# Turning z in 32x32 blocks on VectorE instead of 128x128 tiles on TensorE, in an attention and mixture kernel on one core

## The reference

```python
x = x + attn(layernorm(x))          # 32 heads of 128, 8 key/value heads, chunks of 128 tokens
# per head and chunk: y = (q k^T * decay) v + (q * exp(G)) state ; state = state * dec + k_dec^T v
# y = y / rms(y) * gnorm_w * silu(gate)          -> this is z, up to gnorm_w
# attn = z.reshape(B, L, 32 * 128) @ Wo.T
x = x + ffn(layernorm(x))           # dense 512x512 plus 8 experts of rank 16, softmax weights
```

## Time and profile before

| | |
|---|---|
| median of 3 runs | 1987.81 us (1986.06 to 1990.85) |
| the profiled execution, its own time | 1986.23 us |
| its span | 1984.4 us |
| mean granted TensorE clock | 0.986 of full speed |
| PE busy | 1899.7 us, 96% of the span |
| DVE / ACT / POOL busy | 60% / 38% / 33% |
| DMA | 173.63 MB, 27.2% of 16 engines' time |

### The profile page before, as it was taken

One profiled execution on the slowest core, in us unless ns is written; L12 is line 12 of the kernel. 1 busy time (PEld: TensorE's weight loads), 2 busy tenths in 40 slices (PEclk: granted clock), 3 DMA queues, 4 the chain that ended last, 5 costly groups with the idle time before them and its releaser, 6 DMA issues. The chain is left out here.

```text
span 1984.4 us, 28939 instructions
## 1 busy us (share of the span) xinstructions
PE 1899.7 (96%) x9240; PEld 1514.9 (76%) x9240; DVE 1183.8 (60%) x2208; ACT 759.0 (38%) x2326; POOL 658.1 (33%) x741
## 2 busy tenths in 40 slices
PE   7799999999999999999999899999978999999998
PEld 5588788778877877887788788788766777777775
DVE  7767666766676677666666766766664333333322
ACT  4444444444444444444444444444453121111211
POOL 3443444434444444444444444344410110100100
PEclk9899999999999999999999999999999999999999
DMA  4231222223222222322221232222255322322311
GB/s 150 69 96 59 89 98 70 64 83 100 75 80 98 69 67 84 105 65 92 92 73 61 81 102 72 83 75 68 81 191 176 107 89 70 106 66 92 104 54 43
DMA packets 88389, 173.63 MB, mean 87 GB/s; under 512 B 9392, under 2 KB 15024, under 8 KB 88240
## 3 DMA queue, kind: packets, MB, share of 16 engines
q1 hardware_dynamic: 88240, 171.81, 27.2%
HBM read 133.50 MB, written 38.27 MB: 87 GB/s over the span
## 5 line engine op out<-in xcount | busy, mean ns | idle before, releaser
L82 PE MATMUL p_proj<-wg_hi,shared 128*128 128x512 f32 x1024 | 361.0, 433 | 0.0
L82 PE MATMUL p_proj<-shared,wq_hi 128*128 128x512 f32 x992 | 335.9, 400 | 12.3 <-DVE wq_lo L747 12.3
L111 POOL TENSOR_TENSOR q<-rope_a,rope_b 128x512 f32<-128x512 f32 x128 | 181.5, 1418 | 326.7 <-DVE rope_b L103 326.7
L899 ACT ACTIVATE tanh<-p_proj 128x512 f32<-128x512 f32 x128 | 76.5, 598 | 531.1 <-PE p_proj L82 531.1
L82 PEld LDWEIGHTS p_proj<-wg_hi,shared 128*128 128x128 f32 x1024 | 192.9, 188 | 84.5 <-issue 46.3
L82 PEld LDWEIGHTS p_proj<-shared,wq_hi 128*128 128x128 f32 x992 | 187.1, 189 | 57.7 <-issue 15.1
L82 PE MATMUL p_proj<-wg_lo,shared 128*128 128x512 f32 x512 | 202.2, 395 | 0.0
L82 PE MATMUL p_proj<-shared,wq_lo 128*128 128x512 f32 x496 | 196.3, 396 | 0.0
L101 DVE TENSOR_TENSOR rope_a<-p_proj,cos 128x512 f32<-128x512 f32 x155 | 105.8, 683 | 128.6 <-PE p_proj L82 128.6
L680 PE MATMUL p_y<-v_tok,probs 128*128 128x128 f32 x1024 | 182.3, 275 | 0.0
L82 PE MATMUL p_proj<-shared,wkv_hi 128*128 128x512 f32 x496 | 175.2, 415 | 5.2 <-DVE rope_b L103 4.5
(11 more groups left out here) (181 smaller groups left out, 3795.7 us busy)
## 6 DMA issues: line engine op xcount, KB each, us to landing
g_row<-g_scratch SPq DMA_DIRECT2D x128, 256.0 KB, 3.9
z_scratch<-z_t SPq DMA_DIRECT2D x128, 256.0 KB, 2.8
w_raw<-z_scratch SPq DMA_DIRECT2D x49, 512.0 KB, 6.5
e_row<-e_scratch SPq DMA_DIRECT2D x96, 256.0 KB, 3.6
w_raw<-in_wq_t SPq DMA_DIRECT2D x16, 512.0 KB, 6.0
w_raw<-in_wg_t SPq DMA_DIRECT2D x16, 512.0 KB, 6.0
q<-z_scratch SPq DMA_DIRECT2D x15, 512.0 KB, 6.6
w_raw<-in_wo_t SPq DMA_DIRECT2D x11, 512.0 KB, 4.2
```

Of the source, the lines that this page charges most:

```text
L82: mm = pe.matmul(out, lhs[a], rhs[e], start=(i == 0 and j == 0), stop=(i == len(pairs) - 1 and j == 2))
L111: pool.tensor_tensor(out, keep["rope_a"][:, s, :], keep["rope_b"][:, s, :], ALU.add).then_inc(keep["roped"], 1)
```

## The change

z is no longer turned whole. DVE turns each 32x32 block of the 128x512 tile `z` in place of its four transpositions by PE, and writes it to `z_st` [128, 4 feature blocks, 4 heads, 4 chunks, 32 tokens], which holds a whole step. Partition 32 i + a of `z_st` then holds, for token block i of every chunk, feature a of each feature block. At the start of the next step SP stores it with four transfers of 256 KB, one for each feature block j; each goes to four tiles of `z_dram` and 32 partitions' rows in each. A tile of `z_dram` is now token block u of all four chunks of a batch, so the last stage's tile (b, u) takes 32 tokens of each chunk: its rows of x are read, and of the output written, as four pieces of 32 rows. `z_turn`, `save_z`, the bank `p_zt`, the tile `z_t` and their waits are gone. DVE's turn stands after `rotate_next`, but that of chunk 3 right after `make_z`; before chunk 0's turn DVE waits until the four stores of the step before have landed. ACT's `squares` waits for its own previous `squares`. The last stage's loop body is four tiles, run twice, and SP's is unrolled.

```diff
+BL = 32
+TB = C // BL
-        z_t = sb("z_t", [P, 2, HG, C])
+        z_st = sb("z_st", [P, TB, HG, NC, BL])
...
             def step(g, b, n):                                   # SP
-                    if c > 0:
-                        store_z(g, b, n, c - 1)
-                    elif has_last(n):
-                        store_z(g if b else g - 1, (b - 1) % B, n - 1, NC - 1)
+                    if c == 0 and has_last(n):
+                        store_z(g if b else g - 1, (b - 1) % B, n - 1)
...
-            def store_z(g, b, n, c):
-                sp.wait_ge(zt_saved, NC * n + c + 1)
-                sp.dma_start(z_dram[b * NC + c, :, bass.ds(g * HG, HG), :], z_t[:, c % 2]).then_inc(z_out[c % 2], 16)
+            def store_z(g, b, n):
+                sp.wait_ge(turned, NC * (n + 1))
+                for j in range(TB):
+                    tiles = z_dram[b * TB:(b + 1) * TB, j * BL:(j + 1) * BL, bass.ds(g * HG, HG), :]
+                    sp.dma_start(tiles.rearrange("i a h t -> i a (h t)"),
+                                 z_st[:, j].rearrange("p h c t -> p (h c t)")).then_inc(z_out[j % 2], 16)
...
-            def z_turn(n, c):                                    # PE, and its four calls
-                m = NC * n + c
-                pe.wait_ge(z_set, m + 1)
-                wait_ge(pe, zt_saved, m)
-                for h in range(HG):
-                    t = pe.transpose(p_zt[:, h, :], z[:, h, :], ident[:, :])
-                t.then_inc(zt_done, 1)
...
+            def turn_z(n, c):                                    # DVE
+                dve.wait_ge(z_set, NC * n + c + 1)
+                if c == 0:
+                    for s in range(2):
+                        wait_ge(dve, z_out[s], 16 * TB // 2 * n)
+                dve.transpose(z_st[:, :, :, c, :], z[:, :, :].rearrange("p h (j a) -> p j h a", a=BL)).then_inc(turned, 1)
...
                 if has_last(n):
                     make_z(n - 1, 3)
+                    turn_z(n - 1, 3)
...
                     rotate_next(g, b, n, Q_UNIT[c - 1], c)
+                    turn_z(n, c - 1)
                     make_state(n, b, c)
...
                 rotate_next(g, b, n, Q_UNIT[3], 4)
+                turn_z(n, 2)
...
             def squares(n, c):                                   # ACT
                 act.wait_ge(y_done, NC * n + c + 1)
+                wait_ge(act, squares_set, NC * n + c)
...
-            def save_z(n, c):                                    # ACT, and its four calls
-                m = NC * n + c
-                act.wait_ge(zt_done, m + 1)
-                wait_ge(act, z_out[c % 2], 16 * (2 * n + c // 2))
-                act.activation(z_t[:, c % 2, :, :], p_zt[:, :, :], ACT.Copy).then_inc(zt_saved, 1)
...
+        def batch(step, b, last=False):                          # last stage
+            for u in range(TB):
+                step(b, u, not (last and u == TB - 1))
+
         def tiles(engine, first, step):
             first()
-            step(0, 0, True)
-            step(1, 1, True)
-            with engine.Fori(1, NT // 2 - 1) as pair:
-                step(2 * pair, 0, True)
-                step(2 * pair + 1, 1, True)
-            step(NT - 2, 0, True)
-            step(NT - 1, 1, False)
+            batch(step, 0)
+            with engine.Fori(1, B - 1) as b:
+                batch(step, b)
+            batch(step, B - 1, True)
+
+        def rows(table, b, u):
+            b, u = b + u // TB, u % TB
+            return table.rearrange("(b c t) n -> b c t n", c=NC, t=C)[bass.ds(b, 1), :, u * BL:(u + 1) * BL, :].rearrange(
+                "a c t n -> (a c) t n")
...
-                sp.dma_start(tokens[:, s, :], io["x"][bass.ds(i * P, P), :]).then_inc(x_in[s], 16)
+                sp.dma_start(tokens[:, u % 2, :], rows(io["x"], b, u)).then_inc(x_in[u % 2], 16)
...
-                sp.dma_start(io["out"][bass.ds(i * P, P), :], tokens[:, s, :]).then_inc(out_sent[s], 16)
+                sp.dma_start(rows(io["out"], b, u), tokens[:, u % 2, :]).then_inc(out_sent[u % 2], 16)
```

More of the change, by code:

```diff
@@ L454, in attention_stage @@
         z = sb("z", [P, HG, D])
-        z_t = sb("z_t", [P, 2, HG, C])
+        z_st = sb("z_st", [P, TB, HG, NC, BL])
         p_proj = [pb(f"p_proj{i}") for i in range(2)]
         p_y = [pb(f"p_y{i}") for i in range(2)]
-        p_score, p_cst, p_zt = (pb(n) for n in ("p_score", "p_cst", "p_zt"))
+        p_score, p_cst = (pb(n) for n in ("p_score", "p_cst"))
         p_tok = keep["p_tok"]
@@ L467, in attention_stage @@
         unit_done, score_done, y_done = sem("unit_done"), sem("score_done"), sem("y_done")
-        cst_done, zt_done, tok_done = sem("cst_done"), sem("zt_done"), sem("tok_done")
+        cst_done, tok_done = sem("cst_done"), sem("tok_done")
         probs_set, state_set, qs_set, z_set = sem("probs_set"), sem("state_set"), sem("qs_set"), sem("z_set")
+        turned = sem("turned")
         gate_set, tanh_set, decay_set = sem("gate_set"), sem("tanh_set"), sem("decay_set")
@@ L472, in attention_stage @@
         wk_hi, wv_hi, wq_hi, wg_hi = sem("wk_hi"), sem("wv_hi"), sem("wq_hi"), sem("wg_hi")
-        squares_set, zt_saved, tok_saved = sem("squares_set"), sem("zt_saved"), sem("tok_saved")
+        squares_set, tok_saved = sem("squares_set"), sem("tok_saved")
         masked_set, xw_set = sem("masked_set"), sem("xw_set")
@@ L546, in step @@
                     for s in range(2):
-                        sp.wait_ge(z_out[s], 16 * 2 * (n - 2))
+                        sp.wait_ge(z_out[s], 16 * TB // 2 * (n - 2))
                     sp.wait_ge(y_done, NC * n)
@@ L584, in step @@
                             load_half("wg_t", g + 1, 2)
-            def store_z(g, b, n, c):
-                sp.wait_ge(zt_saved, NC * n + c + 1)
-                sp.dma_start(z_dram[b * NC + c, :, bass.ds(g * HG, HG), :], z_t[:, c % 2]).then_inc(z_out[c % 2], 16)
+            def store_z(g, b, n):
[4 more added lines that the diff above has]
+                                 z_st[:, j].rearrange("p h c t -> p (h c t)")).then_inc(z_out[j % 2], 16)
             steps(sp, first, step)
-            store_z(KVH - 1, B - 1, LAST, NC - 1)
+            store_z(KVH - 1, B - 1, LAST)
         @block.tensor
@@ L705, in step @@
                 gates(g, b, n, 0)
-                if has_last(n):
-                    z_turn(n - 1, 3)
                 mix(n, 0)
@@ L713, in step @@
                     gates(g, b, n, c)
-                    z_turn(n, c - 1)
                     if c == 2:
@@ L722, in step @@
                 first_heads(n, range(2, 4))
-                z_turn(n, 2)
                 if ahead(n):
@@ L732, in _ @@
             steps(pe, first, step)
-            z_turn(LAST, 3)
         @block.vector
@@ L818, in make_z @@
                 dve.wait_ge(srstd_set, m + 1)
-                wait_ge(dve, zt_done, m)
+                wait_ge(dve, turned, m)
                 for h in range(HG):
@@ L871, in _ @@
             make_z(LAST, 3)
+            turn_z(LAST, 3)
         @block.scalar
@@ L985, in step @@
                 make_tanh(g, b, n, 3)
-                save_z(n, 2)
                 if ahead(n):
@@ L999, in _ @@
             squares(LAST, 3)
-            save_z(LAST, 3)
         @block.gpsimd
@@ L1251, in _, with load_x @@
         def _(sp):
-            def load_x(i, s):
-                sp.dma_start(tokens[:, s, :], io["x"][bass.ds(i * P, P), :]).then_inc(x_in[s], 16)
+            def load_x(b, u):
+                sp.dma_start(tokens[:, u % 2, :], rows(io["x"], b, u)).then_inc(x_in[u % 2], 16)
             def first():
@@ L1264, in first, with step @@
                 sp.dma_start(bm[:, :], io["bm_t"]).then_inc(small_in, 16)
-            def step(i, s, has_next):
+            def step(b, u, has_next):
+                i, s = TB * b + u, u % 2
                 load_z(ahead(i)[0:1])
                 if has_before(i):
-                    store(i - 1, 1 - s)
+                    store(b, u - 1)
                 load_z(ahead(i)[1:2])
@@ L1272, in step @@
                     wait_ge(sp, out_sent[1 - s], 8 * (i - s) + 16 * s)
-                    load_x(i + 1, 1 - s)
+                    load_x(b, u + 1)
                 load_z(ahead(i)[2:])
@@ L1279, in load_z, with store @@
                     load_z_piece(sp, keep, i, j, j % SLOTS)
-            def store(i, s):
-                sp.wait_ge(res_set, i + 1)
-                sp.dma_start(io["out"][bass.ds(i * P, P), :], tokens[:, s, :]).then_inc(out_sent[s], 16)
-            tiles(sp, first, step)
-            store(NT - 1, 1)
+            def store(b, u):
+                sp.wait_ge(res_set, TB * b + u + 1)
+                sp.dma_start(rows(io["out"], b, u), tokens[:, u % 2, :]).then_inc(out_sent[u % 2], 16)
+            first()
+            for b in range(B):
+                batch(step, b, b == B - 1)
+            store(B - 1, TB - 1)
             for s in range(2):
```

3 lines of the change are left out of this document (removed).

## The result

The changed kernel takes **1996.74 us** (median of 6 runs, 1994.02 to 1999.12), the kernel before beside it 1987.75 (6 runs, 1986.06 to 1990.85): ratio 1.0045, 95% interval 1.003 to 1.0059. It is slower by some 9 us; the forecast was 1955, and the result lies outside the range 1942 to 1975. The profiled execution took 1998.81 us, its span 1997.0.

A forecast was written before the change was run, and what follows sets the result against it. PE was taken to set the attention stage's pace. From 1986.2 us, -37.0 for slots, -1.5 for the last step, +2 for the loop body and +4 for transfers gave 1953.7, or 1955 as a median; range 1942 to 1975.

The forecast's parts named there:

- the wait of `turn_z(n, 0)`: Attention stage: DVE's new wait for the four z stores would be hidden, with 4.5 us to spare.
- Four DMA engines: Rival: transfers whose DRAM side begins with four use four engines, PE stays whole in attention, 1959 us; chance 0.22.
- Slower: Rival: the store burst holds DVE at `turn_z(n, 0)`, so `gate(1)` misses G2; about 2057 us; chance 0.08.
- slots of 128 x 0.435, less those given back at V: Attention stage: PE's removed turns save 0.435 us a slot, but chunk 2's returns as waiting for `rope_b` in 31 steps.
- given back at `wq_lo` in seven steps: Group-ending steps: chunk 3's saved slot, 0.435 us, is lost again to PE's `wq_lo` wait.
- the sum for 16 engines: The forecast's sum with 0 for the last stage's transfers: 1955 less 4, 1951 us.
- The last step: Step 31: the last turn and copy become one DVE turn and four issues; -1.5 us, bounds 0 and -3.
- The doubled loop body: Last stage: loop body doubles and five back edges become one; +2 us, bounds 0 and 3.4.
- The last stage's transfers: z's stores, x's and output's rows, with DRAM sides beginning with four: +4 us, bounds 0 to +8.

The follow-up runs named there:

- experiments 2 and 6: Changed kernel, four engines kept: 2 moves DVE's turn of chunk 0 later, 1985.62 us; 6 also loads chunk 3's g row before the four stores, 1949.89 us.
- spread_all: Changed kernel with z's stores cut to 32 first on the DRAM side, x's and output's rows each as four transfers of 32 rows; 1947.49 us.
- experiment 7: `spread_all` with DVE making z of chunk 2 after the rotation of unit Q3, in steps that have a next one; 1920.45 us, ratio 0.967.
- experiment 8: `spread_all` with each of DVE's 128 turns made twice, the first result overwritten; 1960.31 us, ratio 0.9876.
- four_in_before: Kernel before, with each chunk's one z store given a DRAM side that begins with four; 1989.13 us, ratio 1.0022.
- g_first_late: Changed kernel, four engines kept, chunk 3's g row loaded before the four stores and DVE's turn of chunk 0 later; 1949.89 us, ratio 0.9817.

## Why the prediction was wrong

**The step that failed** is the wait of `turn_z(n, 0)`, put at nothing in two ways. In the forecast itself the four stores were spread over 16 engines and landed 9.5 us into the step: "Hidden, with 4.5 us to spare." They ran on four, and the turn was let go 19.6 us into the step (709.71, of a step that began at 690.09). And the rival "Four DMA engines" put the price of that case at nothing too: "That pushes `state`, `gate` and `probs`, but PE wants the gate for G2 at about 21.0 (it is set at about 20.4), so PE stays whole, with half a microsecond to spare. The time is the upper end above, 1959." Two things in it were wrong, and a third misled me.

- *The landing.* 12.6 us from the first issue was the estimate (17.9 into the step), 14.1 is the measured one. The pace was right: at 101 GB/s a store takes 2.6 us, against 2.8. The start was slow: from 697 to 699 the queue moved 28 GB/s, which is 1.5 us lost against 101. That the four issues take 3.23 us instead of the 1.4 of the earlier trace rows is no mark of the four engines, for a burst with 32 first took 2.89. At 19.6 the half microsecond is gone.
- *The second hold.* "Behind the burst on SP's queue stand only `load_g(n, 3)` and later, used a chunk further on" was right for sixteen engines, and I carried it over to four without checking. POOL waits for that row 30 times, 7.9 us each, and doing away with DVE's hold alone gives 9 to 11 of 47 us (experiments 2 and 6).
- *Who wants what.* I followed `gate` to G2. PE meets `state(1)` first, for `p_cst` of chunk 2, 20.55 us into a step of `spread_all` (689.57, of 669.02), half a microsecond before G2. This alone changed nothing: with a landing at 17.9 `state(1)` would have been set at about 19.6, in time.

What PE lost by it: it waits for `state` in 24 places, 31.8 us, 3.4 of them in the last step, where `spread_all` waits as long. The other 23 are 28.4 us, and with a lost overlap of 0.25 each (experiment 7) about 34.

The rival "Slower" named this place and this mechanism, with 0.08. Its break-even, a burst of about 13 us, was right: in its terms (from 1.4 us behind the first issue on) the burst took 12.7, and the gain was gone. So was its price: (19.6 - 17.9 - 0.5) x 31 = 37 us, near the 34. Only its pace of 15 us was too slow. The chances were what was badly set. That these transfers run on few engines had no row against it. The Trainium skill, "DMA: Bandwidth & Descriptors", section on why a DMA increments its semaphore by 16, gives four for them; I had cited it and still put 0.22. By that rule the trace agrees: the share of 0.26 is that of four engines, and with 32 in place of four as the slowest dimension it is 0.98 and the hold is gone.

**What was right.** The steps without the stall are the forecast: 42.52 - 3 x 0.435 = 41.21, and 41.24 was measured. Over 31 steps of `spread_all`, copy to copy (82.81 to 1399.14), it is 1316.33 us against 1361.89, 45.6 less. That divides as follows.

| term | forecast | `spread_all` |
|---|---|---|
| slots of 128 x 0.435, less those given back at V | -40.0 | -40.0 (period 41.2) |
| given back at `wq_lo` in seven steps | +3.0 | +6.6 (12.3 to 18.9) |
| first p_score after a back edge, five times | 0 | -12.0 (15.8 to 3.8) |
| sum | -37.0 | -45.4 |

The second row was mis-sized: DVE's turn is on that way too (experiment 8), so 0.94 us a place was lost and not 0.435. The third came unforeseen. In before PE stood 15.8 us at five back edges; no kernel without PE's turns shows this, and at the same places there are five waits of 0.7 to 0.9 us for `rope_b`. `four_in_before`, with the old code for PE, has them still (17.2 us). Why they went, the runs don't say; fewer PE instructions in the body is a guess. So it is in part luck that `spread_all`, 1947.5, lies as near as it does to the 1951 of the sum for 16 engines: 12 us of it come from an effect that the forecast didn't have.

*The last step* was forecast as -1.5 and is a loss: DVE's turn and four issues stand ahead of the stage's start, 5.5 us of wait at the first `p_out` instead of 1.45 (5.1 with 32 rows first, so mostly not the engines' doing). *The doubled loop body* (+2) cost nothing: from the first turn of x to that of the last tile it is 445.10 us in the changed kernel (1531.61 to 1976.71), 445.77 in before. *The last stage's transfers* (+4, 0 to 8): from the first turn of x to the end, 465.4 us in the changed kernel, 462.6 in `spread_all`, 460.8 in before. `g_first_late`, with four engines there, has 466.0. So about +3 for the engines, near the +4 forecast.

In sum the changed kernel is 1947.5 (everything spread) plus some 47 us in the steps, and 2 to 3 at the end. Of the 47, about 34 are PE's waits at `p_cst` with their overlap. Most of the other 13 is the clock. Between the first and the last copy of chunk 0's state, the granted clock stands at 0.50 in 12 stretches of 3.4 us in the changed kernel: behind the five 2.9 us waits for `state`, and behind the seven of 2.6 to 2.7 us for `wq_lo`. `spread_all` has six such stretches, each behind one of its seven waits for `wq_lo`. At half the clock a stretch costs about 1.7 us by my estimate, so six more cost 10; some 3 us stay open. That PE's waits bring the clock down is what the order of the rows suggests; no run tried it alone. Not tried either: two buffers for `z_st`.

## What to carry to other kernels

Before a store is regrouped, write out its DRAM side and look at the slowest dimension: the same bytes, cut along another one, were worth 47 to 48 us here. When several transfers are bundled, there are two victims to follow to the bottleneck engine: who may overwrite the tile, and whose load is issued behind them. Where a forecast rests on half a microsecond of slack in every step, look for the first consumer in the bottleneck's row (here `state`, not `gate`), and give the other outcome a chance to match. Then see what the new order leaves in front of the bottleneck: moving one DVE instruction group behind the rotation gave another 27 us (experiment 7).

## What the runs showed of the hardware

- A 256 KB store whose DRAM side begins with four takes 0.594 us to issue (median), the same bytes 0.356 in before and 0.442 with 32 first. In flight it keeps the DMA share at 0.26 and moves about 101 GB/s; bursts with 32 first reach 0.98. Four in a burst let their tile go 14.1 us after the first issue. The last output store, a single one of that form, ends 6.3 us after its issue, against 2.5 before.
- DVE's 32x32-block transposition of 128x512 fp32 takes 0.712 us, from a permuted view too, near an ordinary 128x512 operation (0.69).
- At the two places looked at, before V and before `p_cst`, a wait of PE costs its named time (0.61, 0.79) and about 0.25 us of overlap: short waits that come every step are worth more than their row says.
- In the changed kernel the granted clock stood at 0.50 for 3.4 us behind each of PE's five waits of 2.9 us at `p_cst` and its seven of 2.6 to 2.7 us for `wq_lo`. It stayed at full speed behind the waits at `p_cst` of 0.5 to 1.7 us in those steps.
